# Attention in a four-layer fp32 network: P V issued whole once a step behind the fourth pair of scores, instead of as two pieces of 256 columns

## What is computed

```python
q, k, v = split_heads(x @ Wq.T), split_heads(x @ Wk.T), split_heads(x @ Wv.T)   # 16 heads of 16
sim = einsum('bhid,bhjd->bhij', q, k) / sqrt(16)          # 4096 x 4096 for each head
sim = where(causal_mask, -large, sim)
exp_sim = exp(sim - max(sim, axis=-1))
attn = exp_sim / (sum(exp_sim, axis=-1) + exp(denom_bias))   # the bias in layer a only
out = einsum('bhij,bhjd->bhid', attn, v)
```

## Time and profile before

| | |
|---|---|
| median of 3 runs | 5369.27 us (5364.77 to 5371.13) |
| the profiled execution: its time, its span | 5370.71 us, 5369.0 us |
| attention core of layer a, within the span | 267 to 1632 us |
| attention core of layer b | 2927 to 4293 us |
| mean granted clock of TensorE | 0.938 of full speed |

### The profile page before, as it was taken

The page is one execution under the profiler, slowest core; times in us unless marked ns, Lnnn a source line. Parts: engine busy times, 40 slices in busy tenths (PEclk is TensorE's granted clock), DMA queues, the critical chain, the costliest instruction groups (busy, mean ns, idle before and its releaser), DMA issues. The chain is left out here.

```text
span 5369.0 us, 100628 instructions
## 1 busy us (share of the span) xinstructions
PE 4616.5 (86%) x40558; PEld 2002.0 (37%) x40558; DVE 4386.0 (82%) x5188; ACT 3145.5 (59%) x5959; POOL 1165.9 (22%) x1140
## 2 busy tenths in 40 slices
PE   5389999999997888699883999999999968886998
PEld 2222223222234444355551222232222344443565
DVE  6199998999876999567743999999998679994777
ACT  2167898889993333234331678888899833332433
POOL 0010001100003555244300000011000125552432
PEclk9699999999997999799985999999999979997999
DMA  3100000000000000400011000000000000004000
GB/s 130 59 2 2 11 16 2 25 2 2 2 2 20 0 0 0 141 1 0 0 69 49 2 2 20 7 2 25 2 2 2 2 18 0 0 0 141 9 12 12
DMA packets 65832, 106.38 MB, mean 20 GB/s; under 512 B 8952, under 2 KB 57208, under 8 KB 61310
## 3 DMA queue, kind: packets, MB, share of 16 engines
q1 hardware_dynamic: 65456, 101.08, 5.8%
HBM read 76.73 MB, written 23.08 MB: 19 GB/s over the span
## 5 line engine op out<-in xcount | busy, mean ns | idle before, releaser
L857 DVE TENSOR_REDUCE b_att_mx<-ps 128x2 f32<-128x1024 f32 (+3 forms) x1152 | 1227.8, 1129 | 192.1 <-PE ps L710 98.3
L857 DVE TENSOR_REDUCE a_att_mx<-ps 128x2 f32<-128x1024 f32 (+3 forms) x1152 | 1227.1, 1129 | 186.3 <-PE ps L710 95.1
L814 ACT ACTIVATE b_att_pt<-ps 128x512 f32<-128x512 f32 (+3 forms) x2304 | 1149.0, 560 | 291.9 <-PE ps L746 261.1
L814 ACT ACTIVATE a_att_pt<-ps 128x512 f32<-128x512 f32 (+3 forms) x2304 | 1149.6, 560 | 288.2 <-PE ps L746 256.6
L746 PE MATMUL ps<-b_att_q,b_att_k 51*128 51x512 f16 (+3 forms) x2304 | 707.8, 368 | 27.5 <-DMA b_att_q<-b_att_mt 26.2
L746 PE MATMUL ps<-a_att_q,a_att_k 51*128 51x512 f16 (+3 forms) x2304 | 705.6, 366 | 27.6 <-DMA a_att_q<-a_att_mt 26.2
L710 PE MATMUL ps<-b_att_k,b_att_q 48*128 48x512 f16 (+3 forms) x2304 | 611.3, 374 | 87.3 <-DMA b_att_k<-b_parts_k 53.5
L710 PE MATMUL ps<-a_att_k,a_att_q 48*128 48x512 f16 (+3 forms) x2304 | 606.9, 372 | 90.0 <-DMA a_att_k<-a_parts_k 53.4
L765 PE MATMUL ps<-b_att_pt,b_v 128*17 128x256 f32 (+1 forms) x8704 | 673.6, 382 | 9.8 <-ACT b_att_osb L801 9.1
L765 PE MATMUL ps<-a_att_pt,a_v 128*17 128x256 f32 (+1 forms) x8704 | 670.7, 380 | 9.9 <-ACT a_att_osb L801 9.2
L746 PEld LDWEIGHTS ps<-b_att_q,b_att_k 51*128 51x128 f16 x2304 | 176.2, 94 | 500.0 <-ACT b_att_pt L814 413.1
(11 more groups left out here) (301 smaller groups left out, 7260.2 us busy)
## 6 DMA issues: line engine op xcount, KB each, us to landing
f_exp_w<-in_expert_w SPq DMA_DIRECT2D x64, 256.0 KB, 5.7
g_exp_w<-in_expert_w SPq DMA_DIRECT2D x64, 256.0 KB, 6.0
x<-in_x SPq DMA_DIRECT2D x1, 4096.0 KB, 19.9
a_parts_q<-a_qkv_cut SPq DMA_DIRECT2D x8, 512.0 KB, 3.2
a_parts_k<-a_qkv_cut SPq DMA_DIRECT2D x8, 512.0 KB, 3.6
a_att_k<-a_parts_k SPq DMA_DIRECT2D x16, 256.0 KB
a_att_q<-a_parts_q SPq DMA_DIRECT2D x16, 256.0 KB
b_parts_q<-b_qkv_cut SPq DMA_DIRECT2D x8, 512.0 KB, 3.6
```

Of the source, the lines that this page charges most:

```text
L814: act.activation(pt[:, s % PT_RING, i, 0:width], ps[:, at:at + width], ACT.Exp, scale=unscale).then_inc(pt_ready, 1)
L857: dve.tensor_reduce(mx[u % 2][:, h:h + 2, t, c], both, AX.X, ALU.max).then_inc(ring_read, 1)
```

## The change

`p_v` loses its second argument and issues the four matmuls of a step at its full width. The loop calls it once a step, behind tile 3 and its row scores, for step s - 1. The call behind tile 1 is gone. The waits are those that the left half had.

```diff
-            def p_v(s, half):
+            def p_v(s):
                 u, kb = STEPS[s]
                 quad, g = UNITS[u]
-                left = BANK - step_width(s)
-                lo, hi = max(left, half * BANK // 2), (half + 1) * BANK // 2
-                first, last = s == FIRST_STEP[u], s + 1 == FIRST_STEP[u + 1]
-                if lo < hi:
-                    if is_diagonal(s):
-                        pe.wait_ge(masked, DIAG_BEFORE[s + 1])
-                    else:
-                        pe.wait_ge(pt_ready, 4 * s + 4)
-                    if first and half == 0:
-                        wait(pe, o_copied, u)
-                    for h in range(4):
-                        mm = pe.matmul(OUT[32 * h:32 * h + VW, lo:hi], v[:, kb, 4 * quad + h, :],
-                                       pt[:, s % PT_RING, h, lo - left:hi - left],
-                                       start=(first and half == 0), stop=(last and half == 1))
-                    if half == 1:
-                        mm.then_inc(pv_done, 1)
+                width = step_width(s)
+                if is_diagonal(s):
+                    pe.wait_ge(masked, DIAG_BEFORE[s + 1])
+                else:
+                    pe.wait_ge(pt_ready, 4 * s + 4)
+                if s == FIRST_STEP[u]:
+                    wait(pe, o_copied, u)
+                for h in range(4):
+                    mm = pe.matmul(OUT[32 * h:32 * h + VW, BANK - width:BANK], v[:, kb, 4 * quad + h, :],
+                                   pt[:, s % PT_RING, h, 0:width], start=(s == FIRST_STEP[u]), stop=(s + 1 == FIRST_STEP[u + 1]))
+                mm.then_inc(pv_done, 1)
...
                     for what in ITEMS_AFTER[4 * s + i + 1]:
                         item(what)
-                    if i == 1 and s >= 2:
-                        p_v(s - 2, 1)
                 if s:
-                    p_v(s - 1, 0)
-            p_v(NS - 2, 1)
-            p_v(NS - 1, 0)
-            p_v(NS - 1, 1)
+                    p_v(s - 1)
+            p_v(NS - 1)
```

## The result

The changed kernel takes 5598.5 us (median of 4 runs, 5594.7 to 5603.0) against 5369.6 us: a ratio of 1.0423, 95% interval 1.0409 to 1.0436, 229 us slower. The direction was forecast, the size was not: 5493 us was predicted, in a range of 5430 to 5560.

The account below looks back on a forecast made before the run. No engine had much slack and TensorE's order decided; with whole P V a closed ring of 2.46 us a step would limit. Terms 35 + 21 + 3 + 3 = 62 us a layer, 124 for two, gave 5493 us, range 5430 to 5560.

Parts of the forecast that it names:

- the ring: Three transposed-tile slots make tile 3, P V, next tile 0, its exp a loop: 2.02 us halved, 2.46 whole.
- five links: Exp end to tile 3 0.05, to P V 0.32, whole P V 1.00, tile 0 to exp 0.49, exp 0.60 us.
- starved reductions: Rival: VectorE's two row-score slots wait through P V, 2.33 us a step against 2.30; 5390 us, chance 0.06.
- the half-hidden ring: Rival: the ring's wait partly lies beside waits already there, half the loss, 62 us; 5431 us, chance 0.10.
- the saving on TensorE: Rival, faster: TensorE's 0.21 us saved a step decides, mainly in the last stretch; 5320 us, chance 0.08.
- no change: Rival: savings at unit changes and in the last stretch cancel the ring's loss; 5369 us, chance 0.04.
- Six turns in 18 are shortened: Narrow steps shorten six ring turns in each 18-step unit, so only two thirds of turns are full and lose.
- hidden as before: Turns beside 256 or 128 wide steps take 2.24 us or less, so lose nothing; beside 384 wide ones, 3 us.
- The three terms 35, 21 and 3 us: Loss a layer in full turns: middle stretch 35 us, last stretch 21, first stretch 3.
- TensorE's clock should stay at 1.00: TensorE's granted clock stays at 1.00 after the change; a drop to half would make the loss larger.
- The unit change: Between units, 10.5 us of copy waits go and up to 14 us come; counted at nothing, some 10 either way.
- Its upper end: Range's top, 5560 us: a little above whole P V at 1.12 us, ring 2.58, 60 us more, 5553.

Follow-up runs that it names:

- e11: Changed kernel with every reduction taken over only the first 128 columns of each block of keys, all matmuls kept: 5433.9 us.
- e1: Changed kernel with whole P V moved: of step s - 2 behind tile 1, not of step s - 1 behind tile 3: 5539.7 us.
- e9_whole_narrow: Kernel before, with P V whole behind tile 3 only where the step or the one after is narrower than 512, halves elsewhere: 5452.4 us.
- e10: Kernel before, with P V whole behind tile 3 only where the step and the one after are both 512 wide, halves elsewhere: 5533.4 us.
- e2_adjacent: Kernel before, with both 256-column pieces of P V of step s - 1 issued one right behind the other, behind tile 3: 5603.1 us.
- e6_norows_whole: Changed kernel without row scores and their reductions, a constant standing for the maxima, still three slots for transposed tiles: 6760.8 us.

## Why the prediction was wrong, point by point

**What bounds the kernel, and the ring: right.** The five links, each read from a row of before, gave 2.46 us; the changed kernel shows 2.45. The cost of whole P V, taken as 1.00, is 0.99. With a 384 piece the ring was to make 2.24, and the median is 2.23. The rivals fall: starved reductions by e11 and e1, the half-hidden ring, the saving on TensorE and no change by the size and sign of the loss.

**"Six turns in 18 are shortened", "hidden as before": the step that failed.** I compared the shortened rings, 2.02 to 2.24, with 2.26, TensorE's time for a full step. But a turn beside a narrow step has less work on every engine and took less before. One such turn in the trace of before, behind a step 256 wide, goes from tile 0 at 967.99 to the next at about 969.61, 1.63 us:

```profile
967.99 0.39 PE L746 MATMUL ps<-a_att_q,a_att_k 51*128 51x512 f16 x1
...
968.52 0.62 PE L765 MATMUL ps<-a_att_pt,a_v 128*17 128x256 f32 x8
969.08 0.39 PE L746 MATMUL ps<-a_att_q,a_att_k 51*128 51x512 f16 x1
...
969.31 0.64 PE L746 MATMUL ps<-a_att_q,a_att_k 51*128 51x512 f16 x2
```

The same step after the change, 1017.63 to 1019.65, is 2.02 us, the ring's 0.05 + 0.32 + 0.56 + 0.49 + 0.60 to the hundredth:

```profile
1017.63 0.39 PE L746 MATMUL ps<-a_att_q,a_att_k 51*128 51x512 f16 x1
...
1018.77 0.39 PE L746 MATMUL ps<-a_att_q,a_att_k 51*128 51x512 f16 x1 [0.32 <-ACT a_att_pt L805]
...
1019.09 0.63 PE L762 MATMUL ps<-a_att_pt,a_v 128*17 128x256 f32 x8
1019.65 0.33 PE L746 MATMUL ps<-a_att_q,a_att_k 51*128 51x384 f16 x1
```

P V of the narrow step is no longer than before. What changed is its place: as a right half it stood behind tile 1 of the following step, outside this ring, and now it stands behind tile 3, in it. I had written that the 64 one-piece steps only move, and had given the move no price. With these turns alone whole, e9_whole_narrow lost 82 us where the sum had 6 for them; about 13 us a layer of it are at the low clock, below. Aligned step by step, the two traces of layer a say (the full turns of the table are those in which no transpose of the maxima stands):

| turns of layer a | count | before, mean us | after, mean us | grew by, us |
|---|---|---|---|---|
| full, steps 0 to 127 | 78 | 2.69 | 2.83 | 11 |
| full, steps 128 to 447 | 213 | 2.29 | 2.47 | 38 |
| full, steps 448 to 575 | 81 | 2.17 | 2.48 | 25 |
| behind a 256 wide step, 128 to 447 | 15 | 1.71 | 2.06 | 5 |
| behind a 384 wide step, 128 to 447 | 15 | 2.03 | 2.24 | 3 |
| every other turn: beside narrow steps, or with a transpose of the maxima | 173 | 2.50 | 2.70 | 35 |
| all | 575 | 2.37 | 2.57 | 117 |

**The full turns: right in kind, short in size.** The three terms 35, 21 and 3 us became 38, 25 and 11 in the change itself. In the middle all 213 turns grew, by 0.18 us on average, where the sum had 177 by 0.20. The first stretch was mis-sized: its 26 full turns with three reductions, counted at nothing, grew by 5 us, and the 52 ordinary ones had a median of 2.26 before, under the 2.40 that I assumed, and grew by 6. e10 finds more still, 163 us for both layers.

**"TensorE's clock should stay at 1.00": not quite.** The prediction put the clock at nothing. The records of the granted clock show 23 us of layer a's core at 0.50 before the change and 70 us after it: the low start that both have, 10 us longer after the change, and seven falls in place of two. One of them:

```profile
1046.00:1050.00 4.00, 3.20 (x36) 0.95 (x32) 3.97 (x5) 2.94 (x8) 1.72 (x6) 1.00 0.13 53
1050.00:1062.00 12.00, 10.43 (x64) 2.85 (x60) 8.87 (x12) 5.01 (x13) 1.27 (x2) 0.57 0.19 66
1062.00:1070.00 8.00, 7.62 (x60) 1.88 (x60) 6.86 (x8) 7.13 (x16) 0.63 (x1) 1.00 0.18 64
```

and a P V in it, 1.77 us for what takes 1.05 elsewhere:

```profile
1059.46 1.77 PE L762 MATMUL ps<-a_att_pt,a_v 128*17 128x512 f32 x8
```

TensorE waits more than before, and most at a change of unit: behind step 128 its records leave 0.39 us of a turn empty there and 0.17 elsewhere, where it was 0.19 and 0.03. All seven falls come one to five steps behind the start of a unit. That the waits bring the clock down is not shown. The 23 steps that touch the low clock are together 17 us longer than the same steps before, of the layer's 117. If every step took the longer of its old time and its ring, the layer would grow by 92 us, 70 of them in full turns and 22 in turns beside narrow steps; with the 17 that leaves 8 unexplained. The prediction had 59 and 3. So the 55 us a layer that its sum lacks are about 19 for turns beside narrow steps, 11 for full turns, 17 at the low clock, and 8 that stay open. No run held the clock fixed, so this share is read from the trace and not tested; the same count gives 13 us a layer in e9_whole_narrow and 15 in e10_whole_full, which would be enough for the 16 us by which the two together exceed the change. In e2_adjacent, with three falls in layer a and not seven, the kernel takes as long as the changed one, so the share varies while the ring's does not.

**The unit change: about nothing, as said.** P V's wait for the copy is 8.3 us in all, 9.2 before, and ScalarE's wait for P V before the copy no longer appears among its waits.

**The range.** Its upper end moved one link (1.12 for P V, which e2 then showed to be 0.99), and its lower end took half of the loss away. Neither moved the claim that the rest is hidden, which held a third of the turns, nor the clock.

## What to carry to other kernels

Where an engine serves a ring of slots and also does long blocks of other work, write down each closed loop, link by link, from the rows of the trace: wake-up, issue, block, latency, consumer. Its sum is a step time that no engine's busy share shows, and here it met the measured turn within 0.02 us. Then compare the loop with what each class of steps takes now, not with the time of the widest one: a loop that is hidden under a full step may be the limit of a narrow one. And work out every ring again for each new place of the block: of the orders tried here, the kernel before is the one in which both rings stay short.

## What was not expected

TensorE at 1.2 GHz for a whole attention core: in e6_norows_whole the granted clock stayed at 0.50 from the idle stretch before layer a's core to the core's end, 2060 us later, with TensorE's records at 90% of the time. Its partners began from the same 0.50 and rose. The Trainium skill (TensorE: Matmul & The Clock Gate, Part 1: The HAM clock gate) says that the gate is set by how busy TensorE has been recently; here the records were busy for 90% of the time and the clock stayed low. At the low clock the same P V fills 1.84 us in place of 0.98, so a kernel at that clock looks busier than it would at the other. What kept the clock down in e6_norows_whole no run tests.

And a switch between scores and P V costs, as an estimate, about 0.09 us on the way in (0.31 from a tile's start to P V's, where two tiles start 0.22 apart) and 0.13 for the piece beyond its columns (2 x 0.56 - 0.99), whether one piece or two adjacent ones stand between: e2_adjacent.
